# The fourth turned state tile of each unit scaled by ScalarE and added by POOL

## The chip, the cores and the metric

One core of one Trainium2 chip. The time is the device time of the whole program in microseconds (us), the median of several runs. Lower is better.

## The reference

The program runs two layers over eight sequences of 1024 rows by 512, all in float32. Layer 0 is a linear attention with a modulated output (not touched here). Layer 1 is a Mamba block on gathered rows. All gather indices are below 512, so only the first 512 positions (one chunk) of each sequence are needed. Cut to the part that matters:

```python
def step(hst, inp):
    dt_t, B_t, C_t, x_t = inp
    dA = jnp.exp(dt_t[:, :, None] * A)                                  # A: 1024 channels x 16 states
    hst = hst * dA + (dt_t * x_t)[:, :, None] * B_t[:, None, :]
    y = jnp.einsum('bds,bs->bd', hst, C_t)                              # the sum over states
    return (hst, y)
...
y = jnp.transpose(ys, (1, 0, 2)) + xm * D_param
y = y * jax.nn.silu(z)
return y @ W_out
```

## The kernel before, in words

Layer 1 (from about 1361 us on) runs in eight **turns**, one for each sequence: turn 0, then a loop whose pass holds two turns (1 and 2, 3 and 4, 5 and 6), then turn 7, then a short end. A turn has 128 **blocks** n = 0 to 127, one for each state s and group j of 128 channels, and 32 **units** q of four blocks each (q = n // 4). In a unit:

- POOL makes the inputs, `u * b_wide`, 128 x 2048, into a ring of four units, `hs` (`inputs`, L1448). Unit q can start once unit q-4 has been turned (transposed) by TensorE, and must be there before block 4q is scanned.
- ScalarE makes the decays of each block, `exp(dt * A)`, into a PSUM bank (`decays`, L1343).
- VectorE scans each block in place along time (`scan`, L1559).
- TensorE turns the four scanned blocks so that time lies on the partitions: four tiles t = 0 to 3 of 128 x 512, four transposes each (`states_turned`, L1165), in two PSUM banks that take turns. Tile t = 2 waits until tile 0 has been read, tile 3 until tile 1 has.
- VectorE multiplies each turned tile by its column of C and adds it to the running sum `acc` (`add_states`, L1586). It does so one unit later: behind the scan of block n = 4q+t stands the addition of unit q-1, tile t. The last unit's four additions stand behind the scan of block 127.

Other work is dealt out over the blocks of a turn. For the sequence before: `y_turned` (L1172) turns `acc` back, which TensorE does in the order j = 0 to 7 at the very start of the next turn and only once all additions of the turn are done; `gate_y` (L1592) on VectorE behind each of the blocks 0 to 7; `project_out` (L1184), `gate_out` (L1603), and on POOL the indirect DMAs `add_y` (L1458) at units 20 to 27. For the sequence after: a gather of rows on POOL at unit 1 (L233), row statistics and `rows_normed` (L260) on VectorE after units 2 and 3, an index step (`next_rows`, L1606) after unit 4, `project_in` (L1124), the conv taps (L1527) at blocks 25 to 56, `project_dt` (L1148) and its four ScalarE steps, and on POOL `add_dt` (L1430) at units 24 and 29 and `dt_x` (L1438) at units 30 and 31. For the sequence itself: the z projections from block 49 on.

Every engine has its own queue and works strictly in the written order. The lines that set it here:

```python
            def turn(b, par, prev, more):          # on POOL
                for q in range(HALVES):
                    inputs(b, q)
                    if more and q >= HALVES - 2:
                        dt_x(b + 1, 1 - par, q - (HALVES - 2))
...
            def y_turned(it, place, j):            # on TensorE
                need(pe, summed, CT * HALVES * it + CT * HALVES)
```

Of the kernel before, what the change touches and what calls it, by code (L numbers as in the profile page):

```python
# [7 lines left out]
ALU = mybir.AluOpType  # L8
# [3 lines left out]
P = 128  # L12
# [800 lines left out]
def layer1(nc, a, g):  # L813
# [14 lines left out]
    with ExitStack() as ctx:  # L828
        def sb(name, shape):
            return ctx.enter_context(nc.sbuf_tensor(name, shape, F32))  # L830
# [17 lines left out]
        b_wide = sb("b_wide", [P, 2, CHUNK])  # L848
        c_t = sb("c_t", [P, 2, CT, STATE])
        gate = sb("gate_wide", [P, DIM])  # L850
        fin = sb("fin", [P, 2, DIM])
# [16 lines left out]
        xm_ready, zs_ready, dt_exp, dt_log, dt_ready, u_ready = (sem(n) for n in ("xm_ready", "zs_ready", "dt_exp", "dt_log", "dt_ready", "u_ready"))  # L868
        da_ready, inputs_ready, scanned, turned, summed, carried = (sem(n) for n in ("da_ready", "inputs_ready", "scanned", "turned1", "summed", "carried"))
        passed = sem("passed1")  # L870
        block = ctx.enter_context(nc.Block())
# [232 lines left out]
        def _(pe):  # L1104
# [52 lines left out]
            def states_turned(it, q, t):  # L1157
# [8 lines left out]
                last.then_inc(turned, 1)  # L1166

            def y_turned(it, place, j):
                need(pe, summed, CT * HALVES * it + CT * HALVES)
                out = claimed(pe, place, "y", j)  # L1170
                for t in range(CT):
                    last = nc.tensor.transpose(out[:, t * P:(t + 1) * P], acc[:, t, j * P:(j + 1) * P], ident[:, :])  # L1172
                last.then_inc(fills(place, "y", j), 1)
# [14 lines left out]
            def turn(b, par, prev, more):  # L1188
                place = turn_place(b)
                def swap_sums(j):  # L1190
                    if prev:
                        y_turned(b - 1, place, j)
                    x_turned(place, j)
# [3 lines left out]
                for q in range(HALVES):  # L1197
                    for t in range(CT):
                        states_turned(b, q, t)
                        if q == 0:  # L1200
# [32 lines left out]
            def first_chunk():  # L1233
                def end():
                    for j in range(KI):
                        y_turned(BATCH - 1, end_place, j)
                    for t in range(CT):
                        project_out(BATCH - 1, end_place, t, range(KI))

                front(0, 0, front_place, 0)  # L1240
                turns(pe, turn, end)
# [24 lines left out]
        def _(act):  # L1266
# [68 lines left out]
            def decays(it, par, k):  # L1335
# [7 lines left out]
                nc.scalar.activation(decay_bank(k)[:, :], dt[:, par, j, :], ACT.Exp, scale=g.decay[:, j, s:s + 1]).then_inc(da_ready, 1)  # L1343

            def turn(b, par, prev, more):
                place = turn_place(b)
                for k in range(3):
                    decays(b, par, k)
                for n in range(BLOCKS):
# [7 lines left out]
                    if n < KI:  # L1357
                        start_sum(place, n)
                    if more:
                        if 17 <= n < 17 + KD:  # L1360
                            norm_modulated(b + 1, 1 - par, place, n - 17)
                        if n in (33, 41, 49, 57):
                            silu_x(place, (n - 33) // 8)
                        if n == 65:
                            keep_xd(b + 1, place)
                        if n == 74:
                            keep_c(1 - par, place)
                        for j, at in enumerate((75, 77, 79, 81, 95, 97, 99, 101)):
# [51 lines left out]
        def _(pool):  # L1420
# [34 lines left out]
            def add_y(b, k, reach):  # L1455
# [56 lines left out]
        def _(dve):  # L1512
# [63 lines left out]
            def add_states(it, par, place, q, t):  # L1576
# [9 lines left out]
                nc.vector.scalar_tensor_tensor(part, state_banks[(CT * q + t) % len(state_banks)][:, :], c_t[:, par, t, s:s + 1], part, ALU.mult, ALU.add).then_inc(summed, 1)  # L1586

            def gate_y(it, place, j):

# [18 lines left out]
            def turn(b, par, prev, more):  # L1608
                place = turn_place(b)
                for q in range(HALVES):  # L1610
                    for t in range(CT):
                        n = CT * q + t
                        scan(b, n)
                        if q:
                            add_states(b, par, place, q - 1, t)
                        if prev:
# [8 lines left out]
                    if more:  # L1625
# [5 lines left out]
                        if q == 4:  # L1631

                            next_rows()
                for t in range(CT):
                    add_states(b, par, place, HALVES - 1, t)

# [77 lines left out]
```

## Time and profile before

| | us |
|---|---|
| median of 3 runs (3575.43 to 3577.82) | 3577.18 |
| span of the profiled execution | 3578.0 |
| VectorE busy | 2649.0 (74%) |
| TensorE matmuls busy | 2949.5 (82%) |
| POOL busy | 1602.0 (45%) |
| ScalarE busy | 1451.0 (41%) |
| mean granted TensorE clock | 0.880 |

The span is the time from the first to the last instruction of the one execution that was profiled; it is within 1 us of the median of the runs. A share of busy time is a mean over both layers; in layer 1 alone VectorE is busy nine tenths and more of nearly every slice. The profile names engines PE (TensorE), DVE (VectorE), ACT (ScalarE), POOL and SP.

### The profile page before, as it was taken

To read this page: it belongs to the slowest core of one execution; us is meant where nothing else is said; L and a number is where in the kernel's file an instruction comes from. 1 tells how busy PE (TensorE), PEld (TensorE's weight loads), DVE (VectorE), ACT (ScalarE), POOL (GpSimd) and SP (SyncE) were. 2 spreads that over 40 slices of the span, in tenths; PEclk is the share of its full clock that TensorE was granted. 3 is DMA by queue.
4 is the path that set the end of the run, shared out by engine and by line. 5 is a ranking of instruction groups with operands and counts; after the bars stand their busy time and mean duration, and the time that the engine had idled before them with its cause. 6 is when DMAs were issued, how large, how long until landed. Compare 5 with 4: busy or idle time off the path is not lost.

```text
span 3578.0 us, 36146 instructions
## 1 busy us (share of the span) xinstructions
PE 2949.5 (82%) x11066; PEld 1633.8 (46%) x11066; DVE 2649.0 (74%) x3437; ACT 1451.0 (41%) x2000; POOL 1602.0 (45%) x539
## 2 busy tenths in 40 slices
PE   7999999999999985777887886886886876887765
PEld 3545455454554433345444444444444444444442
DVE  3444444444443428999999999999999999999993
ACT  1212122221221224564564564564564465565340
POOL 0121111211112105576586586587477477477671
PEclk9999999999999986977977977977977988978877
DMA  5002011020110230101131141141141131131132
GB/s 186 2 23 77 12 64 57 20 76 17 60 62 20 102 96 29 46 21 39 58 96 39 48 107 37 51 104 39 51 104 40 45 101 48 45 100 52 44 94 60
DMA packets 161658, 211.64 MB, mean 59 GB/s; under 512 B 13294, under 2 KB 78962, under 8 KB 161483
## 3 DMA queue, kind: packets, MB, share of 16 engines
q1 hardware_dynamic: 146152, 183.53, 15.9%
q0 software_dynamic: 11776, 25.17, 3.9%
q8 instruction: 76, 1.25, 0.1%
q10 hardware_dynamic: 3554, 0.88, 0.1%
q14 instruction: 100, 0.81, 0.1%
HBM read 167.32 MB, written 42.22 MB: 59 GB/s over the span
## 4 chain that ended last, share of the span: by engine, by line
DVE 33%; issue 14%; PE 12%; ACT 2%; DVEq 1%; POOL 1%; DMA 0%; POOLq 0%; ACTq 0%
DVE hs L1559 18%; DVE acc L1586 11%; PE bank L1165 4%; PE bank L1148 3%; PE bank L1124 2%; DVE xm L1527 2%; PE bank L1184 1%; DVEq L97 1%; PE bank L1154 1%; DVE raw L246 0%; DVE fin L1603 0%; ACT bank L1343 0%; DVE zs L1592 0%; PE bank L1172 0%; ACT acc L1333 0%
## 5 line engine op out<-in xcount | busy, mean ns | idle before, releaser
L1448 POOL TENSOR_TENSOR hs<-u,b_wide 128x2048 f32<-128x2048 f32 x256 | 1169.2, 4571 | 766.8 <-PE bank L1165 615.1
L1559 DVE TENSOR_TENSOR_SCAN hs<-bank,hs 128x512 f32<-128x512 f32 x1024 | 1243.2, 1214 | 8.5 <-issue 6.5
L1343 ACT ACTIVATE bank<-dt,decay 128x512 f32<-128x512 f32 x1024 | 699.3, 690 | 964.0 <-DVE hs L1559 960.9
L1165 PE MATMUL bank<-ident,hs 128*128 128x128 f32 x4096 | 776.8, 328 | 379.4 <-DVE hs L1559 261.2
L1165 PEld LDWEIGHTS bank<-ident,hs 128*128 128x128 f32 x4096 | 580.2, 168 | 950.6 <-issue 473.0
L1586 DVE SCALAR_TENSOR_TENSOR acc<-bank,c_t,acc 128x512 f32<-128x512 f32 x1024 | 747.5, 730 | 59.0 <-PE bank L1165 54.5
L1124 PE MATMUL bank<-h_t,w_in 128*128 128x512 f32 x1024 | 556.4, 631 | 34.3 <-ACT h_t L1274 32.9
L1184 PE MATMUL bank<-w_y,zs 128*128 128x512 f32 x512 | 275.4, 630 | 10.1 <-DVE fin L1603 5.9
L1124 PEld LDWEIGHTS bank<-h_t,w_in 128*128 128x128 f32 x1024 | 180.4, 204 | 130.7 <-issue 120.6
L558 PE MATMUL bank<-z_t,w_k 128*128 128x512 f32 x512 | 221.8, 594 | 5.9 <-ACT z_t L655 5.9
L558 PE MATMUL bank<-w_out,h_t 128*128 128x512 f32 x512 | 221.1, 592 | 0.0
L558 PE MATMUL bank<-rows,z_t 128*128 128x512 f32 x512 | 221.1, 592 | 0.0
L558 PE MATMUL bank<-w_v,z_t 128*128 128x512 f32 x512 | 221.0, 592 | 0.0
L699 POOL TENSOR_TENSOR y_rs<-y_var,mhalf 128x8 f32<-128x8 f32 x8 | 16.0, 2002 | 440.4 <-DVE y_var L186 440.4
L707 POOL TENSOR_TENSOR x_rs<-x_var,mhalf 128x8 f32<-128x8 f32 x7 | 11.5, 1645 | 367.6 <-DVE x_var L186 367.6
L1527 DVE SCALAR_TENSOR_TENSOR xm<-bank,taps,xm 128x511 f32<-128x511 f32 (+2 forms) x192 | 142.8, 744 | 22.4 <-ACT xm L1280 19.8
L712 POOL TENSOR_TENSOR qy<-qy,q_top 128x512 f32<-128x512 f32 x64 | 68.7, 1074 | 199.8 <-DVE q_top L782 199.8
L558 PEld LDWEIGHTS bank<-z_t,w_k 128*128 128x128 f32 x512 | 96.6, 190 | 126.4 <-issue 124.5
L558 PEld LDWEIGHTS bank<-w_out,h_t 128*128 128x128 f32 x512 | 97.2, 190 | 122.8 <-issue 122.8
L558 PEld LDWEIGHTS bank<-w_v,z_t 128*128 128x128 f32 x512 | 97.3, 190 | 122.5 <-issue 122.5
L558 PEld LDWEIGHTS bank<-rows,z_t 128*128 128x128 f32 x512 | 96.7, 190 | 119.1 <-issue 119.1
L749 DVE SCALAR_TENSOR_TENSOR k_t<-bank,k_bias,mask_add 128x512 f32<-128x512 f32 x64 | 48.1, 751 | 139.0 <-PE bank L558 139.0
(150 smaller groups left out, 2983.0 us busy)
## 6 DMA issues: line engine op xcount, KB each, us to landing
w_in<-in_L_cond_W_in SPq DMA_DIRECT2D x128, 256.0 KB, 3.0
b_wide<-b_rows SPq DMA_DIRECT2D x128, 256.0 KB
z<-in_x SPq DMA_DIRECT2D x8, 2048.0 KB, 8.2
res<-in_x SPq DMA_DIRECT2D x8, 2048.0 KB, 8.3
x_rows<-res SPq DMA_DIRECT2D x7, 2048.0 KB, 7.4
fin<-x_rows SPq DMA_DIRECT2D x56, 256.0 KB, 2.9
out<-fin SPq DMA_DIRECT2D x56, 256.0 KB
y_rows<-fin SPq DMA_DIRECT2D x32, 256.0 KB, 3.0
```

The costliest lines, as they stand in the source:

```text
L558: last = nc.tensor.matmul(out[:, :], stationary(k), moving(k), start=(k == 0), stop=(k == blocks - 1))
L712: nc.gpsimd.tensor_tensor(heads, heads, q_top[:, t, :].unsqueeze(2).to_broadcast([P, HEADS, HEAD]), ALU.add).then_inc(q_shifted, 1)
L749: nc.vector.scalar_tensor_tensor(k_t[:, i, half * 512:(half + 1) * 512], banks[(2 * i + half) % MM_RING][:, :], g.k_bias[:, i:i + 1], mask ...
L1124: last = nc.tensor.matmul(work_bank(place, stage, m)[:, :], w_in[:, m % W_IN_RING, k, :], h_t[:, par, k, :], start=(k == 0), stop=(k == KD ...
L1148: nc.tensor.matmul(out[:, :], w_dt[:, j * P:(j + 1) * P], xd[0:RANK, :], start=True, stop=True).then_inc(fills(place, "dt", j), 1)
L1165: last = nc.tensor.transpose(state_banks[n % len(state_banks)][:, j * P:(j + 1) * P], hs[:, q % RING, j, t * P:(t + 1) * P], ident[:, :])
L1184: last = nc.tensor.matmul(out_bank[:, :], zs[:, j, t * P:(t + 1) * P], w_y[:, j, :], start=(j == 0), stop=(j == KI - 1))
L1343: nc.scalar.activation(decay_bank(k)[:, :], dt[:, par, j, :], ACT.Exp, scale=g.decay[:, j, s:s + 1]).then_inc(da_ready, 1)
L1448: nc.gpsimd.tensor_tensor(hs[:, q % RING, :, :], u[:, 4 * half:4 * half + 4, :], b_wide[:, s % 2, :].unsqueeze(1).to_broadcast([P, 4, CHUNK]),
L1527: nc.vector.scalar_tensor_tensor(xm[:, m, back:], bank[:, 0:CHUNK - back], w, xm[:, m, back:], ALU.mult, ALU.add).then_inc(empties(place, ...
L1559: nc.vector.tensor_tensor_scan(block, decay_bank(k)[:, :], block, 0.0, ALU.mult, ALU.add).then_inc(scanned, 1)
L1586: nc.vector.scalar_tensor_tensor(part, state_banks[(CT * q + t) % len(state_banks)][:, :], c_t[:, par, t, s:s + 1], part, ALU.mult, ALU.ad ...
```

## The change

Tile 3 of every unit no longer goes to VectorE. ScalarE scales it out of its PSUM bank into a new SBUF ring of two buffers (`scale_state`, two blocks into the next unit but one step later than VectorE's tile 2), and POOL adds it to `acc` (`pool_state`), for unit q-4 directly ahead of the inputs of unit q. VectorE keeps tiles 0 to 2. `y_turned_apart` waits for both sums. The last four of POOL's additions of a turn stand ahead of the inputs of units 0 to 3 of the next turn. On TensorE the transposes stay in order; only what they wait for changes.

```diff
+SCALED_RING = 2
+DVE_TILES = CT - 1
...
+            def states_turned_apart(it, q, t):
...
+                if t == 0:
+                    need(pe, summed, DVE_TILES * (HALVES * it + q))
+                elif t == 1:
+                    need(pe, state_scaled, HALVES * it + q)
+                else:
+                    need(pe, summed, DVE_TILES * (HALVES * it + q) + t - 1)
...
+            def y_turned_apart(it, place, j):
+                need(pe, summed, DVE_TILES * HALVES * (it + 1))
+                need(pe, state_pooled, HALVES * (it + 1))
...
+            def scale_state(it, par, q):
+
+                s, t = q // 2, CT - 1
+                need(act, turned, CT * HALVES * it + CT * q + t + 1)
+                need(act, state_pooled, HALVES * it + q + 1 - SCALED_RING)
+                nc.scalar.activation(scaled[:, q % SCALED_RING, :], state_banks[(CT * q + t) % len(state_banks)][:, :], ACT.Copy,
+                                     scale=c_t[:, par, t, s:s + 1]).then_inc(state_scaled, 1)
...
+                    if n >= CT and n % CT == CT - 2:
+                        scale_state(b, par, n // CT - 1)
...
+                scale_state(b, par, HALVES - 1)
...
+            def pool_state(it, q):
+
+                t, jg = CT - 1, q % 2
+                part = acc[:, t, jg * 512:(jg + 1) * 512]
+                need(pool, state_scaled, HALVES * it + q + 1)
+                need(pool, state_pooled, HALVES * it + q - 1)
+                nc.gpsimd.tensor_tensor(part, part, scaled[:, q % SCALED_RING, :], ALU.add).then_inc(state_pooled, 1)
+
             def turn(b, par, prev, more):
                 for q in range(HALVES):
+                    if q >= RING:
+                        pool_state(b, q - RING)
+                    elif prev:
+                        pool_state(b - 1, HALVES - RING + q)
                     inputs(b, q)
...
                 def end():
+                    for q in range(HALVES - RING, HALVES):
+                        pool_state(BATCH - 1, q)
...
-                        if q:
-                            add_states(b, par, place, q - 1, t)
+                        if q and t < DVE_TILES:
+                            add_states_apart(b, par, place, q - 1, t)
...
-                for t in range(CT):
-                    add_states(b, par, place, HALVES - 1, t)
+                for t in range(DVE_TILES):
+                    add_states_apart(b, par, place, HALVES - 1, t)
```

On **POOL**, at the end of turn 0 (units 30 and 31; `hs` rows are inputs, `u` rows are `dt_x`, `dt` is `add_dt`), before:

```order
L1430 TENSOR_TENSOR dt<-dt,rows 128x2048
L1448 TENSOR_TENSOR hs<-u,b_wide 128x2048
L1438 TENSOR_TENSOR u<-dt,xm 128x2048
L1448 TENSOR_TENSOR hs<-u,b_wide 128x2048
L1438 TENSOR_TENSOR u<-dt,xm 128x2048
```

and now:

```order
L1469 TENSOR_TENSOR dt<-dt,rows 128x2048
L1506 TENSOR_TENSOR acc<-acc,scaled 128x512
L1487 TENSOR_TENSOR hs<-u,b_wide 128x2048
L1477 TENSOR_TENSOR u<-dt,xm 128x2048
L1506 TENSOR_TENSOR acc<-acc,scaled 128x512
L1487 TENSOR_TENSOR hs<-u,b_wide 128x2048
L1477 TENSOR_TENSOR u<-dt,xm 128x2048
```

Every unit's inputs have one 512-wide addition ahead of them. On **POOL** a few instructions later, at units 1 to 3 of turn 1, around the gather (L99 and L97 rows are register steps), before:

```order
L1448 TENSOR_TENSOR hs<-u,b_wide 128x2048
L97 ISA
L233 DMA rows<-x_rows,idx_in 128x512 x4
L97 REGISTER_ALU
L1448 TENSOR_TENSOR hs<-u,b_wide 128x2048 x2
```

and now:

```order
L1487 TENSOR_TENSOR hs<-u,b_wide 128x2048
L99 ISA
L235 DMA rows<-x_rows,idx_in 128x512 x4
L99 REGISTER_ALU
L1506 TENSOR_TENSOR acc<-acc,scaled 128x512
L99 REGISTER_ALU
L1487 TENSOR_TENSOR hs<-u,b_wide 128x2048
L99 REGISTER_ALU
L1506 TENSOR_TENSOR acc<-acc,scaled 128x512
L1487 TENSOR_TENSOR hs<-u,b_wide 128x2048
```

The last L1506 here is the one that `y_turned_apart` of the turn before waits for; it stands behind the inputs of units 0, 1 and 2, both `dt_x` and the gather. On **VectorE**, blocks 7 to 9 of turn 0 (L1559 and L1612 are the scan), before:

```order
L1559 SCALAR_TENSOR_TENSOR hs<-bank,hs 128x512
L1586 SCALAR_TENSOR_TENSOR acc<-bank,c_t,acc 128x512
L1559 SCALAR_TENSOR_TENSOR hs<-bank,hs 128x512
L1586 SCALAR_TENSOR_TENSOR acc<-bank,c_t,acc 128x512
L1559 SCALAR_TENSOR_TENSOR hs<-bank,hs 128x512
```

and now:

```order
L1651 SCALAR_TENSOR_TENSOR acc<-bank,c_t,acc 128x512
L1612 SCALAR_TENSOR_TENSOR hs<-bank,hs 128x512 x2
L1651 SCALAR_TENSOR_TENSOR acc<-bank,c_t,acc 128x512
```

Two scans now follow each other once a unit.

## Rows read from the trace of the kernel before

**Rows 1.** The page, part 1: busy us, share of the span, instructions of each engine.

```profile
PE 2949.5 (82%) x11066; PEld 1633.8 (46%) x11066; DVE 2649.0 (74%) x3437; ACT 1451.0 (41%) x2000; POOL 1602.0 (45%) x539
```

**Rows 2.** VectorE and ScalarE by line: xcount | busy, mean ns | idle before, releasers.

```profile
L1559 DVE TENSOR_TENSOR_SCAN hs<-bank,hs 128x512 f32<-128x512 f32 x1024 | 1243.2, 1214 | 8.5 <-issue 6.5 <-POOL hs L1448 1.6
L1586 DVE SCALAR_TENSOR_TENSOR acc<-bank,c_t,acc 128x512 f32<-128x512 f32 x1024 | 747.5, 730 | 59.0 <-PE bank L1165 54.5 <-ACT acc L1333 1.7 <-DVE acc L1586 0.9
...
L1343 ACT ACTIVATE bank<-dt,decay 128x512 f32<-128x512 f32 x1024 | 699.3, 690 | 964.0 <-DVE hs L1559 960.9 <-issue 0.7
```

**Rows 3.** Order of time, VectorE: start, duration; unit 0 of turn 0, then turn 3.

```profile
1361.73 4.56 DVE L1559 TENSOR_TENSOR_SCAN hs<-bank,hs 128x512 f32<-128x512 f32 x4
...
2409.00 1.22 DVE L1559 TENSOR_TENSOR_SCAN hs<-bank,hs 128x512 f32<-128x512 f32 x1
2410.13 0.73 DVE L1586 SCALAR_TENSOR_TENSOR acc<-bank,c_t,acc 128x512 f32<-128x512 f32 x1
2410.77 1.22 DVE L1559 TENSOR_TENSOR_SCAN hs<-bank,hs 128x512 f32<-128x512 f32 x1
```

**Rows 4.** Stretches: length, PE, PEld, DVE, ACT, POOL busy (x), PEclk, DMA share, GB/s.

```profile
2181.00:2340.40 159.40, 129.60 (x546) 74.66 (x545) 156.25 (x188) 77.01 (x106) 77.11 (x19) 0.92 0.14 41
2340.40:2365.90 25.50, 22.22 (x66) 11.34 (x65) 21.82 (x26) 13.58 (x22) 18.01 (x6) 0.67 0.37 87
...
2181.00:2453.70 272.70, 215.78 (x854) 124.28 (x854) 262.97 (x307) 149.34 (x201) 177.19 (x49) 0.83 0.24 63
3272.70:3504.30 231.60, 164.00 (x716) 101.25 (x715) 230.40 (x263) 103.52 (x147) 141.72 (x37) 0.80 0.25 66
```

**Rows 5.** Order of time, POOL, turn 3 from unit 24 to turn 4.

```profile
2382.26 1.57 POOL L1458 DMA_INDIRECT fin<-y_rows,idx_first  x1 [0.16 <-issue]
2383.27 5.11 POOL L1448 TENSOR_TENSOR hs<-u,b_wide 128x2048 f32<-128x2048 f32 x1
...
2409.88 4.54 POOL L1448 TENSOR_TENSOR hs<-u,b_wide 128x2048 f32<-128x2048 f32 x1 [2.33 <-PE bank L1165]
2414.37 4.55 POOL L1430 TENSOR_TENSOR dt<-dt,rows 128x2048 f32<-128x2048 f32 x1
2418.85 4.58 POOL L1448 TENSOR_TENSOR hs<-u,b_wide 128x2048 f32<-128x2048 f32 x1
...
2437.13 9.00 POOL L1448 TENSOR_TENSOR hs<-u,b_wide 128x2048 f32<-128x2048 f32 x2
...
2451.08 9.01 POOL L1448 TENSOR_TENSOR hs<-u,b_wide 128x2048 f32<-128x2048 f32 x2
```

**Rows 6.** POOL by line: its 512-wide addition of two tiles in layer 0.

```profile
L702 POOL TENSOR_TENSOR res<-res,out_bias 128x512 f32<-128x512 f32 x64 | 80.0, 1285 | 0.0
```

**Rows 7.** Order of time, VectorE, from block 127 of turn 3 into turn 4.

```profile
2446.23 1.22 DVE L1559 TENSOR_TENSOR_SCAN hs<-bank,hs 128x512 f32<-128x512 f32 x1
...
2448.80 1.60 DVE L1586 SCALAR_TENSOR_TENSOR acc<-bank,c_t,acc 128x512 f32<-128x512 f32 x2 [0.70 <-PE bank L1165]
...
2453.71 0.69 DVE L1592 TENSOR_TENSOR zs<-bank,zs 128x512 f32<-128x512 f32 x1 [0.15 <-PE bank L1172]
```

**Rows 8.** Order of time, TensorE, the same place, and its wait at block 70.

```profile
2447.58 3.99 PE L1165 MATMUL bank<-ident,hs 128*128 128x128 f32 x16 [1.86 <-DVE hs L1559]
2452.56 1.11 PE L1172 MATMUL bank<-ident,acc 128*128 128x128 f32 x4 [0.99 <-DVE acc L1586]
...
2347.04 2.03 PE L1148 MATMUL bank<-xd,w_dt 64*128 64x512 f32 x2 [1.71 <-ACT zs L1292]
```

**Rows 9.** Order of time, VectorE, the start of turn 3 (a new loop pass).

```profile
2179.39 1.23 DVE L1559 TENSOR_TENSOR_SCAN hs<-bank,hs 128x512 f32<-128x512 f32 x1 [2.65 <-issue]
```

**Rows 10.** Order of time, VectorE, turn 4: rows normed, index step.

```profile
2487.66 4.55 DVE L260 TENSOR_SCALAR rows<-rows,mv,rs 128x512 f32<-128x512 f32 x4
...
2499.83 3.36 DVE L1606 TENSOR_SCALAR idx_in<-idx_in 128x8 int32<-128x8 int32 x1
```

**Rows 11.** Order of time, POOL, the same stretch.

```profile
2481.57 8.99 POOL L1448 TENSOR_TENSOR hs<-u,b_wide 128x2048 f32<-128x2048 f32 x2
2498.65 4.51 POOL L1448 TENSOR_TENSOR hs<-u,b_wide 128x2048 f32<-128x2048 f32 x1 [8.09 <-PE bank L1165]
```

More of the change, by code:

```diff
@@ L849, in layer1 @@
         c_t = sb("c_t", [P, 2, CT, STATE])
+        scaled = sb("scaled", [P, SCALED_RING, 512])
         gate = sb("gate_wide", [P, DIM])
@@ L869, in layer1 @@
         da_ready, inputs_ready, scanned, turned, summed, carried = (sem(n) for n in ("da_ready", "inputs_ready", "scanned", "turned1", "summed", "carried"))
+        state_scaled, state_pooled = sem("state_scaled"), sem("state_pooled")
         passed = sem("passed1")
@@ L1166, in states_turned @@
                 last.then_inc(turned, 1)
+            def states_turned_apart(it, q, t):
+                n = CT * q + t
+                if t == 0:
+                    need(pe, scanned, BLOCKS * it + 4 * (q + 1))
+                if t == 0:
+                    need(pe, summed, DVE_TILES * (HALVES * it + q))
[3 more added lines that the diff above has]
+                    need(pe, summed, DVE_TILES * (HALVES * it + q) + t - 1)
+                for j in range(4):
+                    last = nc.tensor.transpose(state_banks[n % len(state_banks)][:, j * P:(j + 1) * P], hs[:, q % RING, j, t * P:(t + 1) * P], ident[:, :])
+                last.then_inc(turned, 1)
+            def y_turned_apart(it, place, j):
+                need(pe, summed, DVE_TILES * HALVES * (it + 1))
+                need(pe, state_pooled, HALVES * (it + 1))
+                out = claimed(pe, place, "y", j)
+                for t in range(CT):
+                    last = nc.tensor.transpose(out[:, t * P:(t + 1) * P], acc[:, t, j * P:(j + 1) * P], ident[:, :])
+                last.then_inc(fills(place, "y", j), 1)
             def y_turned(it, place, j):
@@ L1191, in swap_sums @@
                     if prev:
-                        y_turned(b - 1, place, j)
+                        y_turned_apart(b - 1, place, j)
                     x_turned(place, j)
@@ L1198, in turn @@
                     for t in range(CT):
-                        states_turned(b, q, t)
+                        states_turned_apart(b, q, t)
                         if q == 0:
@@ L1235, in end @@
                     for j in range(KI):
-                        y_turned(BATCH - 1, end_place, j)
+                        y_turned_apart(BATCH - 1, end_place, j)
                     for t in range(CT):
@@ L1586, in add_states, with add_states_apart @@
                 nc.vector.scalar_tensor_tensor(part, state_banks[(CT * q + t) % len(state_banks)][:, :], c_t[:, par, t, s:s + 1], part, ALU.mult, ALU.add).then_inc(summed, 1)
+            def add_states_apart(it, par, place, q, t):
+                s, jg = q // 2, q % 2
+                if q < 2:
+                    for j in (4 * jg + 2, 4 * jg + 3):
+                        need(dve, *read_by(place, "init", j))
+                else:
+                    need(dve, summed, DVE_TILES * (HALVES * it + q - 2) + t + 1)
+                need(dve, turned, CT * HALVES * it + CT * q + t + 1)
+                part = acc[:, t, jg * 512:(jg + 1) * 512]
+                nc.vector.scalar_tensor_tensor(part, state_banks[(CT * q + t) % len(state_banks)][:, :], c_t[:, par, t, s:s + 1], part, ALU.mult, ALU.add).then_inc(summed, 1)
             def gate_y(it, place, j):
```

## The prediction

> **What bounds the kernel now.** The shares of the page [rows 1] name PE, but they are a mean over two layers. The groups by line say more: the 1024 scans cost VectorE 1243 us with 8.5 us of idle time ahead of them, the 1024 additions 747 us with 59 us [rows 2]. The stretches of one turn, taken from its first `gate_y` to the next turn's (turn 3, 2181.0 to 2453.7), show VectorE busy 263.0 of 272.7 us; up to the scan of block 70 (2340.4) it is 156.3 of 159.4 [rows 4]. Only between blocks 71 and 82 is it held up: 21.8 of 25.5 us, with PE busy 22.2 at a mean clock of 0.67. Layer 1 is VectorE's.
>
> Then the place where turns meet. From the inputs of unit 29 (2409.88, which still waited 2.33 us) POOL works without a gap until 2460.09 [rows 5]: it hides behind VectorE, but has nothing to give. The end of a turn reads: last scan done at 2447.45, last addition at 2452.4, `y_turned` at 2452.56, `gate_y` at 2453.71 [rows 7, 8], 6.2 us after the scan. Everything of the next turn on VectorE but one scan stands behind that `gate_y`.
>
> **The change on VectorE.** A scan and an addition take 1.77 us from start to start (2409.00 to 2410.77); scans without one between follow at (4.56 - 1.21) / 3 = 1.12 us [rows 3]. So each removed addition is worth 0.65 us: 256 of them 166 us, 20.2 a turn (31) plus one behind the last block. A bare unit goes from 7.09 to 6.44 us. Where VectorE already waits, a step is worth less: of the 16 steps up to block 70 (10.4 us) I take off 1.0, because 3.15 us of that stretch are not VectorE's [rows 4]; 9.4 are left.
>
> **ScalarE.** 256 scalings out of PSUM. An exponential of the same size takes 0.69 [rows 2]; with overlap I take 0.65 between starts. ScalarE is busy 149 of 272.7 us [rows 4] and 32 x 0.65 = 21 us fit; the order of instructions shows no further table load. Behind a scaling the decays queue, three to four blocks ahead of the scan; its own wait (tile 3 turned) costs at most a few us of that lead. I cost it at nothing, hidden by the lead and, late in the turn, by POOL; without these up to 0.65 a unit. POOL can start its addition 1.4 us after the scan of the block at which the scaling stands (one exponential, one scaling, a signal).
>
> **POOL.** The new addition has no row in layer 1. Near it is layer 0's addition of two 512-wide tiles in place: 80.0 / 64 = 1.25 us [rows 6]. Bounds: a quarter of the 2048-wide operation, 1.13, and 1.4. I take 1.25, as form and size are the same. Inputs take 4.53 us; an `add_y` with them 6.28 (2382.26 to 2388.55), so 1.75 for itself; `add_dt` 4.55; `dt_x` 4.5; the gather 5.0 (2446.13 to 2451.08) [rows 5]. A unit from 20 to 27 thus costs POOL 4.53 + 1.25 + 1.75 = 7.5 us, more than VectorE's 6.44: POOL falls behind from unit 20 on, and is not caught up until `y_turned`, which now waits for POOL's 32nd addition. That one stands behind both `dt_x`, the inputs of units 0 to 2 and the gather.
>
> The chain, from the scaling at block 70 (POOL's unit 20) to that addition: 16 additions 20.0, 15 inputs 68.0, 8 `add_y` 14.0, 2 `add_dt` 9.1, 2 `dt_x` 9.0, gather 5.0: **125.1 us**. A turn is then: 159.4 - 9.4 up to block 70, + 1.4, + 125.1, + 1.3 (from the addition's end to `gate_y`, as 2452.4 to 2453.71) = **277.8 us for 272.7**. What VectorE gains is turned into a wait: some 10 us ahead of block 124 for inputs, some 18 us at `gate_y`.
>
> **The sum.** Turns 1, 3 and 5: +5.1 each. Turns 2 and 4 begin the next turn with a loop pass that costs 2.65 us before its first scan [rows 9], which vanishes in the wait: +2.5 each. Turn 6: its successor has no gather, 5.0 less: +0.1. Turn 0 has no `add_y`; POOL waits again at unit 29 (block 106) and needs from there 7 additions 8.8, 6 inputs 27.2, `add_dt` 4.5, `dt_x` 9.0, gather 5.0 = 54.5, with 1.4 and 1.3 57.2, where before 21 steps of 1.77 and 6.2 made 43.4: +13.8; saved up to there 25 x 0.65 = 16.3, less 2.2 for steps that wait, plus the 3.7 of blocks 71 to 82 (see below): -4.0. Turn 7: POOL has neither `dt_x` nor gather and keeps up (83 us for units 20 to 31, against 87): 20.2 saved, less a new stall where PE runs at half clock. There the first tile of a unit comes 1.35 us after the scan (2447.45 to 2448.80 [rows 7]), VectorE now wants it after 1.04: 0.31 x 31 units x 0.4 (clock 0.80 [rows 4]) = 3.8; -16.4. At the end the last tile is turned 4.1 us after the scan, scaled and added by 6.2, where `y_turned` could start at 4.8: +1.4.
>
> Two VectorE steps meet POOL. `rows_normed` takes 4.55 us for four tiles, the index step 3.36; the first tile of the one, and the other, only get through when POOL's inputs end (2490.56, 2503.16) [rows 10, 11]. With POOL's queue moved, and each engine served in the order of asking, I get for `rows_normed` 0.3 (the end of an input) + 0.5 + 1.25 (an addition) + 0.5 + 4.5 (a whole input) + 0.9 = 7.9 us (+3.4), for the index step 0.8 (the end of an addition) + 0.3 = 1.1 (-2.3): +1.1 a turn, +7.7 in seven.
> The Trainium skill ("SBUF — State Buffer", on the two separate sides) says that VectorE's two-port operations and POOL share a port pair as an exclusive lock, held for the whole instruction. By that rule the trace agrees for these two steps, and scans and additions, which read PSUM, stay free; without the lock both steps would cost under 2.2 us and the sum 7.7 less.
>
> Sum: 3 x 5.1 + 2 x 2.5 + 0.1 - 4.0 - 16.4 + 1.4 + 7.7 = **+9.1 us** against the profiled 3578.0 and the median 3577.18 alike (0.8 apart): **3586 us**. About 0.2% (7 us) is what a measurement of this kernel can tell from no change.
>
> **Rivals.**
> *PE's clock.* In the above, blocks 71 to 82 run at VectorE's pace. Before, PE waited 1.71 us there for ScalarE and the stretch ran at a mean clock of 0.67 [rows 4, 8]. That wait gets shorter by one step, so I think the clock stays up, but if it falls again, nothing is saved from 71 to 82, and POOL's chain starts at block 82 instead (13 additions 16.3, 12 inputs 54.4, 5 `add_y` 8.8, 9.1, 9.0, 5.0 = 102.5): 150.0 + 25.5 + 1.4 + 102.5 + 1.3 = 280.7, 2.9 more in each of six turns and 3.7 in turn 0: +30, 3607. For it: it fell there in every turn before. Chance 0.25.
> *VectorE wins the collisions.* It asks while POOL's input is still running; if all four tiles of `rows_normed` pass in one go they take 2.2 (-2.4), the index step ends early (-2.3 to -3.2): -5.2 a turn instead of +1.1, and with POOL's addition at 1.13 as well (0.12 less, 16 additions in each of six turns: -11) the time is 3577 + 1.4 - 36 - 11 = 3531; half of both is likelier, 3555. This is the faster side: it decides from the point where more than 1.1 + 0.3 us a turn of the collisions goes away. Chance 0.17.
> *The addition on POOL is dear.* At 1.4 us, 16 x 0.15 x 6 = +14, 3600; with the clock low 3620. Chance 0.08.
> *POOL has room after all*, because its spans in the profile are rough: VectorE keeps nearly all, 166 less the stalls, about 3430. Against it: POOL's rows follow each other without a gap for 50 us already now. Chance 0.03.
> The Trainium skill ("GPSIMD Engine Reference", § 4.1 Engine selection) advises against an elementwise addition of two tiles here, since VectorE is about twice as fast. By that rule the move could only pay where POOL is idle; its measured 2048-wide addition, 4497 ns, a quarter of which is 1.12, would take 2 us off each of my turns.
>
> **How the numbers follow.** My own case 0.47 (3575 to 3600), the others as given. The likeliest is 3586. 8 in 10 lie between 3555 (half of the collisions gone) and 3614 (clock low, with a little more). Faster by over 0.2%: 0.17 + 0.03 + 0.02 of my own case = 0.22. Within 0.2%: 0.23, nearly all from my own case. Slower: 0.55.
>
> **What would show it.** VectorE's additions 768, scans and additions of unchanged length, units of 6.44 in the second half of turn 7. POOL's new line x256 at 1.25, and POOL without a gap from unit 20 to 22 of a turn until `y_turned`. A wait of about 18 us of `gate_y` for `y_turned`, and of `y_turned` for POOL, in seven places, and waits of scans for POOL's inputs ahead of block 124. VectorE idle some 36 us a turn. A turn of 278 us, turn 7 some 16 us shorter. Wrong if POOL has gaps in units 20 to 31, if `gate_y` waits less than 10 us, or if turn 7 gains nothing.

## The result, and the profile after

| us | before | after |
|---|---|---|
| median | 3576.3 (3575.36 to 3577.82, 4 runs) | 3596.77 (3595.09 to 3599.9, 4 runs) |
| span of the profiled execution | 3578.0 | 3595.9 |

The ratio of the times is **1.0054, 95% interval 1.0039 to 1.0068**: slower by half a per cent, where +9 us (3586) was forecast; the two spans differ by 17.9 us.

Part 1 of the page of the changed kernel (busy us, share of the span, instructions), which answers to [rows 1]:

```profile
PE 2906.4 (81%) x11066; PEld 1626.9 (45%) x11066; DVE 2486.4 (69%) x3181; ACT 1599.5 (44%) x2256; POOL 1917.9 (53%) x795
```

VectorE (DVE) is relieved of 163 us of work, and the profiled execution is 18 us longer. The groups by line (count | busy us, mean ns | idle us before, with releasers), which answer to [rows 2, 6]:

```profile
L1612 DVE TENSOR_TENSOR_SCAN hs<-bank,hs 128x512 f32<-128x512 f32 x1024 | 1228.0, 1211 | 51.1 <-POOL hs L1487 31.1 <-ACT bank L1371 19.9
L1651 DVE SCALAR_TENSOR_TENSOR acc<-bank,c_t,acc 128x512 f32<-128x512 f32 x768 | 561.1, 731 | 100.9 <-PE bank L1185 97.4 <-ACT acc L1361 2.5
L1506 POOL TENSOR_TENSOR acc<-acc,scaled 128x512 f32<-128x512 f32 x256 | 360.9, 1410 | 398.3 <-ACT scaled L1378 398.2
L1378 ACT ACTIVATE scaled<-bank,c_t 128x512 f32<-128x512 f32 x256 | 172.9, 676 | 124.1 <-POOL acc L1506 66.3 <-PE bank L1185 56.9
L1657 DVE TENSOR_TENSOR zs<-bank,zs 128x512 f32<-128x512 f32 x64 | 43.5, 684 | 105.2 <-PE bank L1193 105.0
L262 DVE TENSOR_SCALAR rows<-rows,mv,rs 128x512 f32<-128x512 f32 x32 | 52.2, 1690 | 0.0
L1671 DVE TENSOR_SCALAR idx_in<-idx_in 128x8 int32<-128x8 int32 x8 | 2.0, 253 | 0.0
```

Scans and additions are as long as before. Idle time ahead of the scans went from 8.5 to 51.1 us, ahead of the additions from 59 to 101, and `gate_y` (L1657) alone waits for 105 us. The same groups of the kernel before, for the two steps that meet POOL:

```profile
L260 DVE TENSOR_SCALAR rows<-rows,mv,rs 128x512 f32<-128x512 f32 x32 | 33.2, 1097 | 0.0
...
L1606 DVE TENSOR_SCALAR idx_in<-idx_in 128x8 int32<-128x8 int32 x8 | 23.4, 2919 | 0.0
```

`rows_normed` costs 19.0 us more, the index step 21.4 less.

Turn 3 of the changed kernel by stretches (from `gate_y` to block 70, to 82, to 106, to 127, to the next `gate_y`, and the whole; columns as in [rows 4]):

```profile
2187.60:2337.30 149.70, 124.47 (x545) 73.64 (x545) 145.63 (x172) 86.11 (x121) 94.96 (x34) 0.93 0.14 43
2337.30:2361.70 24.40, 21.48 (x63) 10.58 (x63) 19.80 (x21) 15.32 (x25) 23.37 (x10) 0.65 0.38 87
2361.70:2405.40 43.70, 37.39 (x134) 20.79 (x133) 39.20 (x43) 37.24 (x49) 40.70 (x17) 0.73 0.49 115
2405.40:2444.80 39.40, 23.17 (x94) 14.26 (x92) 34.29 (x37) 25.98 (x33) 39.18 (x14) 0.68 0.22 60
2444.80:2467.40 22.60, 5.10 (x22) 4.18 (x23) 3.50 (x5) 3.18 (x5) 21.52 (x11) 0.50 0.19 59
2187.60:2467.40 279.80, 211.61 (x854) 123.45 (x854) 242.42 (x276) 167.83 (x232) 219.73 (x82) 0.80 0.23 62
```

The stretch up to block 70 is 9.7 us shorter than in [rows 4] (159.4), and the turn 7.1 longer (279.8 for 272.7): all of the gain, and more, lies between the last scan and `gate_y`, 22.6 us where it was 6.3. VectorE is busy in 3.5 of them, POOL in 21.5. In order of time on VectorE, TensorE and POOL, where [rows 5, 7, 8] had the place before:

```profile
2451.19 1.22 DVE L1612 TENSOR_TENSOR_SCAN hs<-bank,hs 128x512 f32<-128x512 f32 x1 [2.31 <-ACT bank L1371]
2467.38 0.69 DVE L1657 TENSOR_TENSOR zs<-bank,zs 128x512 f32<-128x512 f32 x1 [14.97 <-PE bank L1193]
```

```profile
2466.23 1.11 PE L1193 MATMUL bank<-ident,acc 128*128 128x128 f32 x4 [17.35 <-POOL acc L1506]
```

```profile
2338.93 1.28 POOL L1506 TENSOR_TENSOR acc<-acc,scaled 128x512 f32<-128x512 f32 x1
...
2354.55 1.26 POOL L1506 TENSOR_TENSOR acc<-acc,scaled 128x512 f32<-128x512 f32 x1 [0.56 <-ACT scaled L1378]
...
2364.22 1.28 POOL L1506 TENSOR_TENSOR acc<-acc,scaled 128x512 f32<-128x512 f32 x1 [2.22 <-ACT scaled L1378]
...
2397.13 1.56 POOL L1497 DMA_INDIRECT fin<-y_rows,idx_first  x1 [0.16 <-issue]
2398.13 1.86 POOL L1506 TENSOR_TENSOR acc<-acc,scaled 128x512 f32<-128x512 f32 x1
2399.36 5.12 POOL L1487 TENSOR_TENSOR hs<-u,b_wide 128x2048 f32<-128x2048 f32 x1
...
2464.84 1.26 POOL L1506 TENSOR_TENSOR acc<-acc,scaled 128x512 f32<-128x512 f32 x1
```

`y_turned` (L1193) starts when the addition at 2464.84 ends; that is the 32nd, and from the one at 2364.22 to it POOL waits for no other engine. The engine that hid behind VectorE now sets the turn's end.

### The profile page after: what moved, and what is told of

It reads as the page before. It is cut to its first block, busy times and chain, and to the rows that moved or that the text cites. A ratio compares the mean times of both kernels' runs of the same rounds, so it can differ in the third digit from the quotient of the medians.

```text
span 3595.9 us, 37440 instructions
## 1 busy us (share of the span) xinstructions
PE 2906.4 (81%) x11066; PEld 1626.9 (45%) x11066; DVE 2486.4 (69%) x3181; ACT 1599.5 (44%) x2256; POOL 1917.9 (53%) x795
## 3 DMA queue, kind: packets, MB, share of 16 engines
q8 instruction: 76, 1.25, 0.1%
## 4 chain that ended last, share of the span: by engine, by line
issue 19%; POOL 17%; DVE 14%; PE 7%; DMA 4%; ACT 3%; DVEq 0%; POOLq 0%; SPq 0%; ACTq 0%
POOL hs L1487 13%; DVE hs L1612 7%; DVE acc L1651 4%; POOL acc L1506 2%; PE bank L1185 2%; DMA fin<-y_rows,idx_first 2%; PE bank L1128 1%; PE bank L1212 1%; PE bank L1158 1%; DVE rows L262 1%; POOL fin L1497 1%; DMA b_wide<-b_rows 1%; POOL rows L235 1%; DMA out<-fin 1%; POOL dt L1469 1%
## 5 line engine op out<-in xcount | busy, mean ns | idle before, releaser
L1612 DVE TENSOR_TENSOR_SCAN hs<-bank,hs 128x512 f32<-128x512 f32 x1024 | 1228.0, 1211 | 51.1 <-POOL hs L1487 31.1
L1487 POOL TENSOR_TENSOR hs<-u,b_wide 128x2048 f32<-128x2048 f32 x256 | 1194.0, 4664 | 115.3 <-DVE u L1604 115.3
L1185 PE MATMUL bank<-ident,hs 128*128 128x128 f32 x4096 | 768.0, 325 | 352.2 <-DVE hs L1612 230.4
L1651 DVE SCALAR_TENSOR_TENSOR acc<-bank,c_t,acc 128x512 f32<-128x512 f32 x768 | 561.1, 731 | 100.9 <-PE bank L1185 97.4
L1506 POOL TENSOR_TENSOR acc<-acc,scaled 128x512 f32<-128x512 f32 x256 | 360.9, 1410 | 398.3 <-ACT scaled L1378 398.2
L1212 PE MATMUL bank<-w_y,zs 128*128 128x512 f32 x512 | 263.9, 606 | 3.5 <-DVE fin L1668 2.5
L1378 ACT ACTIVATE scaled<-bank,c_t 128x512 f32<-128x512 f32 x256 | 172.9, 676 | 124.1 <-POOL acc L1506 66.3
L709 POOL TENSOR_TENSOR x_rs<-x_var,mhalf 128x8 f32<-128x8 f32 x7 | 11.5, 1646 | 367.3 <-DVE x_var L188 367.3
```

Of the source, the lines that this page charges most:

```text
L1185: last = nc.tensor.transpose(state_banks[n % len(state_banks)][:, j * P:(j + 1) * P], hs[:, q % RING, j, t * P:(t + 1) * P], ident[:, :])
L1212: last = nc.tensor.matmul(out_bank[:, :], zs[:, j, t * P:(t + 1) * P], w_y[:, j, :], start=(j == 0), stop=(j == KI - 1))
L1378: nc.scalar.activation(scaled[:, q % SCALED_RING, :], state_banks[(CT * q + t) % len(state_banks)][:, :], ACT.Copy, scale=c_t[:, par, t, s ...
L1487: nc.gpsimd.tensor_tensor(hs[:, q % RING, :, :], u[:, 4 * half:4 * half + 4, :], b_wide[:, s % 2, :].unsqueeze(1).to_broadcast([P, 4, CHUNK]),
L1506: nc.gpsimd.tensor_tensor(part, part, scaled[:, q % SCALED_RING, :], ALU.add).then_inc(state_pooled, 1)
L1612: nc.vector.tensor_tensor_scan(block, decay_bank(k)[:, :], block, 0.0, ALU.mult, ALU.add).then_inc(scanned, 1)
```

## The experiments

Three questions: what the wait at the turn's end costs, and what of it is POOL's additions as such; what PE's clock has to do with it; and what the meetings of VectorE and POOL cost. Each kernel is compared with the kernel before, run on the same chip; the ratios are of this kind. Differences in us between two experiments are between medians of different chips, on which the kernel before took 3574.4 to 3578.3 us. Layer 1 starts between 1356.2 and 1361.7 us in the 14 profiled executions, the latest in the kernel before, although no edit touches layer 0: differences between two spans hold that scatter.

**e1: the gather two units later.** POOL's chain ends at the 32nd addition, ahead of the inputs of unit 3; behind it the gather's 5.0 us are out of the chain.

```diff
-                        if q == 1:
+                        if q == 3:
                             gather(b + 1, b + 1, 0)
```

> The changed kernel with the gather on POOL moved from unit 1 to unit 3, so that it stands behind POOL's last addition of the turn before and no longer ahead of it. If POOL's chain (the additions, inputs, dt_x and gather ahead of the 32nd addition) sets when y_turned starts, the gather's 5.0 us leave the chain in six turns: 3597 - 30 = 3567 us, the wait of gate_y at those turns 5 us shorter, and turn 6 to 7 unchanged. If the time was lost to ScalarE's scalings or to TensorE's clock between blocks 71 and 82, nothing moves by more than 3 us.

Measured 3558.07 us, ratio 0.9954 (0.9937 to 0.9970): 39 us less than the changed kernel (36 by the two ratios), 9 less than expected. Turn 3, blocks 71 to 82 and last scan to `gate_y`:

```profile
2321.70:2343.20 21.50, 16.36 (x67) 8.52 (x66) 19.39 (x23) 15.13 (x25) 21.20 (x9) 0.92 0.35 87
...
2426.50:2444.10 17.60, 5.05 (x22) 4.13 (x23) 3.48 (x4) 3.19 (x6) 17.60 (x7) 0.60 0.05 16
```

The end is 5.0 us shorter in each of turns 0 to 5, 30 us in all, as the gather says, and unchanged in turn 6. The rest goes with the clock: between blocks 70 and 82 it stayed at 0.92 for 0.65, the stretch took 21.5 us for 24.4, and POOL's chain ran from block 70 without a wait for a scaled tile (2.8 us in turn 3 of the changed kernel). That the clock did it alone is not shown: the mean clock of this profiled execution was 0.892 and that of the other three 0.883, at times within 3 us of its own. A turn is 273.1 us; by the prediction's working without the gather it would be 277.8 - 5.0 + 1.1 = 273.9.

**e2: no additions on POOL.** The scaling stays, the semaphore is counted up without work; the fourth tile of each unit is missing from the sum.

```diff
-                nc.gpsimd.tensor_tensor(part, part, scaled[:, q % SCALED_RING, :], ALU.add).then_inc(state_pooled, 1)
+                pool.sem_inc(state_pooled, 1)
```

> The changed kernel with POOL's 256 additions left out (POOL waits for the scaled tile and signals), so the fourth tile of each unit is missing in the sum. It prices POOL's additions alone; ScalarE's scalings and VectorE's saving stay. POOL's chain from the scaling at block 70 falls from 125 to about 105 us, about what VectorE needs for the same blocks, so gate_y waits at most 2 us more than before the change: some 14 us a turn less than before, 3465 us (3455 to 3480). If instead ScalarE's scalings or the clock took the gain, it stays near 3597 or above 3540.

Measured 3459.78 us, 0.9675 (0.9659 to 0.9691). In turns 0 to 6 `gate_y` follows the last scan by 6.3 to 6.8 us (10.4 where a loop pass begins), and its wait is gone:

```profile
L1657 DVE TENSOR_TENSOR zs<-bank,zs 128x512 f32<-128x512 f32 x64 | 42.8, 674 | 5.0 <-PE bank L1193 5.0
```

The two profiled executions differ by 128 us (the one of e2 was 10 us above the median of its runs). The turns' ends give 100 of them, and blocks 107 to 127, where scans had waited for inputs, 20. So nearly all of the 137 us between the medians are waits for POOL's chain with the additions in it; that their place in it counts, and not their number, is for e3 to show.

**e3, e4: only the first 20, or 24, units of a turn.** The later units keep four tiles on VectorE; the last pooled addition of a turn then stands well ahead of its end.

```diff
-DVE_TILES = CT - 1
+POOLED = tuple(range(20))
...
-                        if q and t < DVE_TILES:
+                        if q and (t < CT - 1 or q - 1 not in POOLED):
```

> Only units 0 to 19 give their fourth tile to ScalarE and POOL; units 20 to 31 go back to VectorE. POOL has no addition behind unit 23 and the turn's end is as before the change. By the theory VectorE keeps what it saves up to unit 20: about 11 us in each of turns 0 to 6 and 10 in turn 7, 87 in all: 3490 us (3480 to 3505), gate_y 6.2 us after the last scan. If the loss in the changed kernel came from something in the first 20 units, the time stays above 3550.

> As the last, with units 0 to 23. POOL's additions then reach to unit 27, inside the stretch where it also has add_y, but the chain to the inputs of unit 31 keeps about 10 us of slack and y_turned does not wait for POOL. VectorE's four further steps are worth little, since the stretch from unit 23 to 25 is held by TensorE and ScalarE: 3478 us (3468 to 3495), up to 15 below the kernel with units 0 to 19. If POOL's load between units 20 and 27 is what costs, it is slower than that one.

Measured 3476.62 (0.9722, 0.9706 to 0.9739) and 3472.48 us (0.9716, 0.9699 to 0.9732). The second is in its range; the first is 3 us below its own, and in turns 0, 2, 4 and 6 of its trace blocks 71 to 82 take 21.5 us at a clock of 0.92, for 24.6 to 25.4 before. With 96 of the 256 moves undone the kernel is 120 us faster than the changed one. Up to block 70 a turn takes the same 149 to 150 us in both: the gain of the other moves had been there all along, and was lost at the turn's end.

**e5: a ScalarE copy two blocks earlier.** In the changed kernel PE waits 1.33 us for ScalarE a few blocks behind 70 (1.71 before [rows 8]), and then its clock falls; the copy that competes there moves.

```diff
-                    for m, at in enumerate((58, 69, 73, 90, 91, 106, 110, 114)):
+                    for m, at in enumerate((58, 69, 71, 90, 91, 106, 110, 114)):
```

> The changed kernel with one ScalarE step (the copy of z projection 2 out of PSUM, for which TensorE waits at block 70) moved from block 73 to block 71. It asks whether TensorE's clock in blocks 71 to 82 is what lies between the likeliest case of the prediction (3586) and the measured 3597. If so, the granted clock of that stretch is about 0.9 instead of 0.65 in turns 1 to 6, the stretch takes 21.5 us instead of 24.4, POOL's chain starts at block 70 and a turn takes about 2 us less: 3597 - 12 = 3585 us (3578 to 3590). If POOL's chain is alone to blame, the stretch gets shorter but the time stays within 3 us of 3597.

Measured 3579.69 us, 1.0015 (1.0001 to 1.0029): 17 us less than the changed kernel, in the range. Blocks 71 to 82 of turn 3:

```profile
2332.00:2354.70 22.70, 19.55 (x67) 9.90 (x66) 19.63 (x23) 15.20 (x25) 22.26 (x10) 0.77 0.35 84
```

The clock is 0.77 for 0.65 and the turn 276.5 us for 279.8, with the same 22.6 us at its end. The 0.9 that was expected came in turn 1 alone; turns 2 to 6 have 0.77. The wait for ScalarE is gone, but soon after it PE waits longer for a scan, and the clock falls at 2342.4, for 10.2 us where it was 17.1:

```profile
2340.38 0.65 PE L1185 MATMUL bank<-ident,hs 128*128 128x128 f32 x4 [2.07 <-DVE hs L1612]
```

So this place, the wait with the clock that follows it, is worth 3 us a turn; the edit does not part the two. One of its ten executions took 3599.67 us, as long as the changed kernel, at a mean clock of 0.870 for 0.885 to 0.888 in the nine others.

**e6, e7: 24 units, with a pause of POOL, and both edits.** In e6 POOL waits for the four normed tiles ahead of the inputs of unit 6; in e7 the copy of e5 is moved as well.

```diff
                 for q in range(HALVES):
+                    if more and q == 6:
+                        need(pool, g.normed, CT * (b + 2))
```

> Units 0 to 23 on ScalarE and POOL, and POOL waits ahead of its unit 6 until VectorE has done rows_normed. If VectorE's four tile steps alternate with POOL's operations, each waiting for the other's whole instruction, the four take about 2.1 to 2.8 us instead of 7.2: 4.5 us a turn in seven turns, 3472 - 31 = 3441 us (3435 to 3450). POOL has the slack for it in unit 6. If the four steps are slow for another reason (their operands, the clock), nothing is gained and the wait costs POOL up to 3 us a turn.

> The last kernel with ScalarE's copy moved to block 71 as well. Where the clock stays up in blocks 71 to 82 already, nothing is gained; in some turns it did not. 0 to 10 us less than the last: 3436 us (3426 to 3445).

Measured 3447.15 (0.9636, 0.9620 to 0.9652) and 3444.85 us (0.9635, 0.9619 to 0.9651). Both are in their ranges. The pause gives 25 us: `rows_normed` alone falls by 36.0 us (51.9 in e4, 15.9 in e6), but in turns 1 to 6 blocks 71 to 82 take 24.2 to 24.3 us at a clock of 0.72, where e4 had 21.0 to 21.5 in four of them. Moving the copy gives nothing more here: the same blocks take 22.7 to 24.3 us in e7, at clocks of 0.71 to 0.77.

**e8: the additions as such.** The kernel before, with 256 additions of the same size on a buffer of their own, at the places of `pool_state`; nothing waits for them.

```diff
+                    if q >= RING or prev:
+                        spare_add(HALVES * b + q - RING)
                     inputs(b, q)
```

> The kernel before the change with POOL also making 256 additions of the same size on a spare buffer, at the places of the changed kernel's; VectorE keeps all four tiles, ScalarE has no scalings and y_turned does not wait for POOL. By the theory POOL's load alone costs little: at VectorE's old pace of 7.09 us a unit the inputs of unit 31 still come in time, gate_y stands 6.2 us after the last scan, and the time is 3574 us plus 0 to 15 (rows_normed up to 3 us a turn slower, the index step up to 3 faster). If POOL's additions as such slow VectorE or hold its inputs back, it is 3590 or more.

Measured 3597.02 us, 1.0052 (1.0036 to 1.0069). **A miss**: without a wait for them the additions cost the same 20 us as the change. The equality is chance: the change pays at the turns' ends, and this kernel in `rows_normed`. By groups:

```profile
L260 DVE TENSOR_SCALAR rows<-rows,mv,rs 128x512 f32<-128x512 f32 x32 | 54.9, 1774 | 0.0
...
L1620 DVE TENSOR_SCALAR idx_in<-idx_in 128x8 int32<-128x8 int32 x8 | 22.5, 2807 | 0.0
```

`rows_normed` has 21.7 us more, the index step 0.9 less; units 20 to 31 and the turn's end are as before (6.26 us from scan to `gate_y` in turn 3). What VectorE does there, and POOL beside it, in order of time:

```profile
2495.03 6.57 DVE L260 TENSOR_SCALAR rows<-rows,mv,rs 128x512 f32<-128x512 f32 x3
```

```profile
2493.56 1.26 POOL L1466 TENSOR_TENSOR spare<-spare 128x512 f32<-128x512 f32 x1
2494.79 4.67 POOL L1450 TENSOR_TENSOR hs<-u,b_wide 128x2048 f32<-128x2048 f32 x1
2499.43 1.44 POOL L1466 TENSOR_TENSOR spare<-spare 128x512 f32<-128x512 f32 x1
2508.04 4.52 POOL L1450 TENSOR_TENSOR hs<-u,b_wide 128x2048 f32<-128x2048 f32 x1 [7.17 <-PE bank L1167]
```

The last three of four tiles take 6.57 us while POOL does inputs and an addition: the tiles and POOL's instructions go by turns. The added instruction does not only take its own time; it fills the pause in which three tiles passed unhindered.

**e9 to e11: the pause of POOL in three kernels** (28 units; the changed kernel; the kernel before), to see how the two costs add up.

> Units 0 to 27 pooled, units 28 to 31 with all four tiles on VectorE, and POOL made to wait for the normed rows ahead of the inputs of unit 6. Theory (the fourth tile costs only where y_turned waits for it): POOL's last addition is that of unit 27, issued at unit 31 ahead of that unit's inputs, so the turn ends on the last scan as with 24 units pooled; VectorE is spared 4 more additions of 0.65 us a turn (2.6) but may wait some 2 us for the inputs of unit 31: 3440 us, within 10, so between 17 below and 3 above the 3447 of the run with 24. Rival (POOL has no room for four more in the last twelve units): VectorE waits for inputs in units 28 to 31 for over 5 us a turn, and the time is 3470 or more.

> The changed kernel with POOL waiting for the normed rows ahead of the inputs of unit 6. Theory (two costs that add up): VectorE's four normed tiles fall from 7.2 to about 2.1 us in seven turns, POOL starts that unit some 2 us later and has room before unit 20, so the turn's end is unchanged: 3596 - 7 x 4.5 = 3565 us, within 10, and the wait of y_turned for the additions stays at 17 us. Rival (the pause moves POOL's whole chain): the wait for the additions grows by what the normed rows give, and the time stays within 5 us of the changed kernel's.

> The kernel before with the same wait of POOL. Theory: the four normed tiles fall from 4.5 to about 2.1 us in seven turns, nothing else moves: 3576 - 17 = 3560 us, within 6. Rival (the collision moves to the index step or to a scan wait for later inputs): the time stays within 5 us of 3576.

Measured: e9 3444.93 us, 0.9631 (0.9614 to 0.9647), in its range, as good as 24 units and no better: scans wait 27.2 us for inputs (L1504 is `inputs`), where in e6 it was 2.3.

```profile
L1637 DVE TENSOR_TENSOR_SCAN hs<-bank,hs 128x512 f32<-128x512 f32 x1024 | 1228.4, 1211 | 27.3 <-POOL hs L1504 27.2
```

and e6:

```profile
L1637 DVE TENSOR_TENSOR_SCAN hs<-bank,hs 128x512 f32<-128x512 f32 x1024 | 1236.1, 1216 | 11.4 <-issue 9.1 <-POOL hs L1504 2.3
```

e10 3550.87 us, 0.9923 (0.9906 to 0.9940), and e11 3549.26 us, 0.9922 (0.9905 to 0.9938): both below their ranges (within 10 and within 6), by 14 and 11 us from the expected value. The groups of e10:

```profile
L262 DVE TENSOR_SCALAR rows<-rows,mv,rs 128x512 f32<-128x512 f32 x32 | 16.3, 569 | 0.0
...
L1673 DVE TENSOR_SCALAR idx_in<-idx_in 128x8 int32<-128x8 int32 x8 | 6.4, 795 | 0.0
```

and of e11:

```profile
L260 DVE TENSOR_SCALAR rows<-rows,mv,rs 128x512 f32<-128x512 f32 x32 | 15.3, 541 | 0.0
...
L1608 DVE TENSOR_SCALAR idx_in<-idx_in 128x8 int32<-128x8 int32 x8 | 22.1, 2764 | 0.0
```

In e10 the normed tiles give 35.9 us (52.2 to 16.3; I had counted 31), the index step takes back 4.4, and 22.6 us still lie between scan and `gate_y`. The two costs add up: the pause delays nothing at the turn's end, because POOL has room early in a turn. The spans differ by 47.0; of the further 15, 2.6 are the start of layer 1; the others, half of them ahead of block 70, are not accounted for. In e11 the normed tiles give 17.9, as forecast; the spans differ by 32.8, and the further 15 are partly a start of layer 1 that is 5 us earlier (1356.55 for 1361.73, not an effect of this edit in layer 1), and partly a clock of 0.86 or 0.87 in blocks 71 to 82 of three turns (22.8 us; with the clock at 0.66 or 0.67 they took up to 25.5). **With the pause in both kernels the change makes no difference that these runs can tell** (0.9923 and 0.9922). Of the 19 us by which the pause helps the changed kernel more, the two steps explain 12: `rows_normed` gives 18 more there (35.9 for 17.9), the index step 6 less (it gets 4.4 longer there, and 1.3 shorter in the kernel before). The rest is not told apart.

**e12: the additions as such, with the pause.** e8 and the edit of e6 together.

> The kernel before with the 256 spare additions on POOL, and POOL made to wait for the normed rows ahead of unit 6. Theory (the spare additions cost VectorE only the turns that POOL's instructions take between its four normed tiles): normed rows at about 1.9 us a turn as without the additions, units 20 to 31 unchanged, and the time is that of the kernel before with the wait alone, 3549 us, within 6. Rival (the additions slow VectorE or PE elsewhere too, and the 20 us of the run without the wait are only partly the normed rows): 3560 us or more.

Measured 3557.07 us, 0.9946 (0.9929 to 0.9962): between the two expectations, 2 us above the theory's range.

```profile
L260 DVE TENSOR_SCALAR rows<-rows,mv,rs 128x512 f32<-128x512 f32 x32 | 15.2, 538 | 0.0
...
L1622 DVE TENSOR_SCALAR idx_in<-idx_in 128x8 int32<-128x8 int32 x8 | 28.7, 3589 | 0.0
```

The normed tiles are at 15.2 us, as said; against e8 the time is 40 us lower. Of the 7.8 us above e11, 6.6 are the index step, which now meets POOL at a worse place (28.7 for 22.1). The additions cost VectorE what these two steps wait, and some 1 us that is not told apart from the scatter.

## Why the prediction was nearly right, and where not

The sign, the mechanism and the range (3555 to 3614) held; the forecast itself was 11 us low. Point by point:

- **VectorE's saving**: 768 additions of unchanged length. In turn 7, where VectorE sets the pace, three units of four steps take 6.43, 6.71 and 6.70 us (second scan pairs at 3490.83, 3497.26, 3503.97, 3510.67), for 6.44 forecast, the longer ones because the tile is late from TensorE:

```profile
3490.83 2.33 DVE L1612 TENSOR_TENSOR_SCAN hs<-bank,hs 128x512 f32<-128x512 f32 x2
...
3497.26 2.33 DVE L1612 TENSOR_TENSOR_SCAN hs<-bank,hs 128x512 f32<-128x512 f32 x2
3499.75 0.75 DVE L1651 SCALAR_TENSOR_TENSOR acc<-bank,c_t,acc 128x512 f32<-128x512 f32 x1 [0.16 <-PE bank L1185]
...
3516.17 0.75 DVE L1651 SCALAR_TENSOR_TENSOR acc<-bank,c_t,acc 128x512 f32<-128x512 f32 x1 [1.15 <-PE bank L1185]
```

- **ScalarE at nothing**: right for the turns that POOL ends. Its scalings wait 66 us for POOL, and the scan of block 0 of the next turn, which stands behind the last additions, waits 1.4 to 4.7 us for its decays (2.31 at 2451.19), which ScalarE makes behind the turn's last scaling; that one had waited 5.0 us for POOL to empty a buffer of the ring. Up to `gate_y` both lie in POOL's shadow.
- **POOL's chain**: forecast 125.1 us from the addition at block 70 to the end of the 32nd. Measured 2338.93 to 2466.10, 127.2, of which 2.8 are two waits for scaled tiles: 124.4 us of work. The 1.25 us for the addition, taken from [rows 6], stood at 1.22 between starts. The step to `gate_y` was 1.28 for 1.3. VectorE's idle time came out (37.4 us in turn 3, "some 36"), its places less so: in turns 1 to 6 the scans of blocks 120 and 124 wait 4.6 to 4.9 us for inputs, where "some 10" was said, and the first `gate_y` behind these turns waits 10.1 to 15.0 where "about 18" was; waits for turned tiles and for the decays hold the rest.
- **PE's clock: the step that failed** was "That wait gets shorter by one step, so I think the clock stays up". The wait did get shorter, 1.71 to 1.33 us, and in turns 1 to 6 the clock fell all the same (0.65 to 0.72). In the changed kernel it is full (2.4 GHz) up to 2344.6 in turn 3, then half (1.2) for 17.1 us; in e1, with the same 1.33 us ahead of it, it was full until 2338.3, most of the stretch. The wait in the changed kernel, and the two halves of its stretch:

```profile
2343.22 1.12 PE L1152 MATMUL bank<-xd,w_dt 64*128 64x512 f32 x2 [1.33 <-ACT zs L1320]
```

```profile
2337.30:2344.60 7.30, 4.95 (x25) 2.60 (x25) 7.30 (x9) 4.58 (x7) 7.30 (x3) 1.00 0.28 80
2344.60:2361.70 17.10, 16.53 (x41) 7.98 (x39) 12.50 (x13) 10.74 (x18) 16.07 (x8) 0.50 0.43 90
```

and e1 up to its fall:

```profile
2321.70:2338.30 16.60, 11.46 (x53) 5.72 (x51) 16.60 (x20) 12.72 (x22) 16.30 (x8) 1.00 0.29 75
```

  The rival that got a chance of 0.25 is what happened: its working, 150.0 + 25.5 + 1.4 + 102.5 + 1.3 = 280.7, reads 149.7 + 24.4 + 2.5 + 101.9 + 1.3 = 279.8 in the trace of turn 3 (2361.70 to 2364.22 is the 2.5, from there to 2466.10 the 101.9). Only turn 0 kept its clock, where I had the rival add 3.7 us.
- **The meetings with POOL**: `rows_normed` forecast at 7.9 us a turn, measured 7.2; the index step at 1.1, measured 0.14 in most turns. Net -2.4 us for the program (+19.0 - 21.4), forecast +7.7: this term was 10 us too high, and hid that the clock had gone the other way. That the tiles alternate with POOL's instructions, the least certain part of the working, is what e8 shows.
- **Turn 0**: forecast -2.9 with the meetings, measured +1.3 (269.94 to 271.24). The end from block 106 came out (+13.7 for +13.8). Too high was, above all, "saved up to there 25 x 0.65": blocks 83 to 106 gave 1.2 us and not the 4 that six steps are worth; in turns 0 to 6 of every kernel here that stretch takes 43 us or more, with PE busy 37 of 44 in the changed one.
- **Turn 7 and the end**: forecast -15.0 together, measured -11.5 (237.07 to 225.12, and 0.5 behind it). The tiles were later than the 0.31 us of my estimate, as the two waits above show, and from the last scan to `gate_y` it took 7.4 us for 5.5.

In sum, against +9.1: turns 1 to 6 +30.6 (forecast +27.0), turn 0 +1.3 (-2.9), turn 7 and the end -11.5 (-15.0), the start of layer 1 -2.5 (none): +17.9. The distance of 9 us is a difference of larger errors. Apart from the meetings the sum was 21 us too low (11 in turns 1 to 6, 6.5 in turn 0, 3.5 behind them); the meetings and the start of layer 1 took 12.6 of that back. That the forecast came so near is partly luck.

## What to carry to other kernels

Work that is moved to an engine with idle time on average is only free if that engine has idle time where the moved work falls due; the last item of a stage decides, so leave the items near a hand-over on the engine that does the hand-over. Moving the first 24 of 32 units and none of the rest turned a loss of 0.5% into a gain of 2.8%, and with a pause of POOL into 3.6%. The Trainium skill ("GPSIMD Engine Reference", § 4.1 Engine selection) puts POOL's elementwise addition at about twice VectorE's time; the trace agrees (1.22 us between starts, for the 0.65 of VectorE's multiply and add of the same size), and the move paid where POOL was idle all the same. Look next at the short instructions that share something with the busy engine: a pause at the right unit, one line, gave the kernel before 0.8%, more than the change itself cost.

## What was not expected of the hardware

- In these runs VectorE's tensor-scalar steps and POOL's two-input steps take turns, one instruction each. In the changed kernel four such tiles of some 0.53 us took 7.17, and the shortest and longest of one tile were:

```profile
L262 DVE TENSOR_SCALAR rows<-rows,mv,rs x8: 534/1080/4712, 2219.9 to 2506.4; 128x512 f32<-128x512 f32 x8
```

  (min, median, max in ns, of two turns). With POOL paused (e10, three turns) it reads 532/536/681. The Trainium skill ("SBUF — State Buffer", on the two separate sides) has VectorE's two-port operations and POOL share a port pair as an exclusive lock for a whole instruction; the 4.71 us of one tile beside inputs of 4.67 agree.
- A POOL addition issued behind an indirect DMA, or in a row of instructions after one, is reported at 1.83 to 1.86 us for 1.26 to 1.28, and inputs at 5.1 for 4.5, while the spacing of starts stays at 1.23 (2398.13 to 2399.36): the reported ends overlap the next start, and the line's mean of 1.41 overstates its cost.
- Why the clock fell while VectorE scanned block 75 in one kernel and block 81 in another, whose sole difference is the place of a gather 60 blocks and more ahead of it, was not settled; nor why it kept up in turn 0.
